# An eight-image convolution and attention kernel on one Trainium2 core: the next image's normalisation moved to GpSimd, and parts of the attention put in another order

## What is computed

```python
x = x + L0(gn(x));  x = x + L1(gn(x))
# L0: N = 2 bottlenecks, C = 256, 4 heads of 64, 1024 positions
t = cbs(x, cv1_w, cv1_bn, 0)                    # 1x1, batch norm, silu
ys = [t[:, :C], t[:, C:]]
for i in range(N):
    yi = ys[-1]
    z = cbs(yi, m_cv1_w[i], m_cv1_bn[i], 1)     # 3x3
    # attention: logits = q.(k + r) / 8, softmax over 1024 keys, times v
    z = bot_attention(z, m_qkv_w[i], m_rw[i], m_rh[i])
    z = silu(bn_eval(conv2d(z, m_cv2_w[i], 0), m_cv2_bn[i]))
    ys.append(yi + z)
return cbs(concatenate(ys, axis=1), cv2_w, cv2_bn, 0)
```

## Time and profile before

| | |
|---|---|
| median of 3 runs | 3366.75 us (3364.51 to 3368.51) |
| the profiled execution, its own time | 3367.39 us |
| its span | 3365.7 us, 1.7 us less than its time |
| mean granted TensorE clock | 0.981 of full speed |
| image 2 begins and ends | 983.65 to 1380.17 us of the span |

### The profile page before, as it was taken

The page is one execution under the profiler, slowest core; times in us unless marked ns, Lnnn a source line. Parts: engine busy times, 40 slices in busy tenths (PEclk is TensorE's granted clock), DMA queues, the critical chain, the costliest instruction groups (busy, mean ns, idle before and its releaser), DMA issues.

```text
span 3365.7 us, 61219 instructions
## 1 busy us (share of the span) xinstructions
PE 3077.0 (91%) x27308; PEld 1574.1 (47%) x27308; DVE 1934.3 (57%) x2575; ACT 1616.3 (48%) x1870; POOL 873.6 (26%) x664
## 2 busy tenths in 40 slices
PE   3779989999999989999999899999899999998997
PEld 3534444454544545444444445445454454445453
DVE  5537565474755656465654757546564657537474
ACT  1315475172733646255651738326462456517382
POOL 1114141041411322132411414113231324014041
PEclk8889999999999999999999999999999999999998
DMA  4200000200011000100001000110001000000001
GB/s 143 73 26 29 1 29 26 78 2 29 11 49 46 2 29 20 57 29 1 30 26 66 14 29 8 38 60 2 29 20 57 29 1 30 26 29 27 1 8 44
DMA packets 35896, 105.61 MB, mean 31 GB/s; under 512 B 12976, under 2 KB 15024, under 8 KB 32944
## 3 DMA queue, kind: packets, MB, share of 16 engines
q1 hardware_dynamic: 35632, 101.69, 8.5%
HBM read 80.18 MB, written 21.50 MB: 30 GB/s over the span
## 4 chain that ended last, share of the span: by engine, by line
PE 70%; DVE 11%; ACT 7%; issue 7%; POOL 4%; DMA 1%; SPq 0%; POOLq 0%; DVEq 0%
PE ps_u L676 42%; PE ps_u L835 12%; DVE row_max L1192 4%; PE ps_o L857 3%; PE ps_o L858 3%; ACT wide L981 3%; PE ps_o L859 3%; PE ps_u L809 3%; ACT ps_u L981 2%; DVE probs L1202 1%; POOL wide L1300 1%; PE ps_u L695 1%; POOL y_pad L1300 1%; ACT probs L985 1%; DVE qk L1181 1%
## 5 line engine op out<-in xcount | busy, mean ns | idle before, releaser
L676 PE MATMUL ps_u<-y_pad,w_c 128*128 128x512 f16 x3456 | 789.5, 386 | 0.0
L1192 DVE TENSOR_REDUCE row_max<-ps_u 128x2 f32<-128x1024 f32 x512 | 619.8, 1221 | 219.6 <-PE ps_u L809 219.3
L1320 POOL TENSOR_TENSOR probs<-wide,probs 128x1024 f16<-128x1024 f32 x224 | 477.2, 2130 | 501.7 <-ACT probs L985 492.4
L676 PEld LDWEIGHTS ps_u<-y_pad,w_c 128*128 128x128 f16 x3456 | 331.3, 98 | 425.2 <-issue 24.2
L1002 DVE SCALAR_TENSOR_TENSOR wide<-wide 128x512 f32<-128x512 f32 x256 | 175.5, 688 | 608.9 <-ACT wide L903 606.7
L835 PE MATMUL ps_u<-qk 64*128 64x512 f16 x3072 | 425.2, 383 | 73.3 <-DVE probs L1202 24.9
L902 ACT ACTIVATE wide<-ps_u,par_m_t 128x512 f32<-128x512 f32 x128 | 99.3, 775 | 758.2 <-PE ps_u L676 758.2
L857 PEld LDWEIGHTS ps_o<-v_ext,probs 128*128 128x128 f16 x4096 | 375.7, 96 | 143.5 <-issue 129.0
L857 PE MATMUL ps_o<-v_ext,probs 128*128 128x65 f16 x4096 | 431.2, 193 | 0.0
L858 PE MATMUL ps_o<-v_ext,probs 128*128 128x64 f16 x4096 | 429.0, 195 | 0.0
L859 PE MATMUL ps_o<-v_ext,probs 128*128 128x65 f16 x4096 | 426.5, 191 | 0.0
(11 more groups left out here) (180 smaller groups left out, 3788.9 us busy)
## 6 DMA issues: line engine op xcount, KB each, us to landing
w_c<-w_c_dram SPq DMA_DIRECT2D x15, 2304.0 KB, 8.9
xn<-in_x_dram SPq DMA_DIRECT2D x32, 512.0 KB, 5.9
o_nat<-in_x_dram SPq DMA_DIRECT2D x64, 256.0 KB, 2.6
out_dram<-qk SPq DMA_DIRECT2D x32, 512.0 KB, 2.7
w_c_dram<-w_c SPq DMA_DIRECT2D x2, 2304.0 KB, 8.0
qk<-in_L_conv_m_cv_w_dram SPq DMA_DIRECT2D x2, 1152.0 KB, 6.9
probs<-in_L_conv_m_cv_w_dram SPq DMA_DIRECT2D x2, 1152.0 KB, 11.1
probs<-in_L_conv_cv_w_dram SPq DMA_DIRECT2D x2, 1024.0 KB, 11.8
```

Source lines behind the costliest of these rows:

```text
L676: ins = e.matmul(o, lhsT, rhs, start=start and k == 0, stop=stop and k == len(pairs) - 1)
L1192: e.reduce_max(row_max[:, g % 2, :, it, half], ps_u[:, use.slot:use.slot + 2, :], axis=AX.X).then_inc(*dve_max.up(i, b, g, half, it))
L1320: e.tensor_tensor(p_part(s, 1), wide[:, w.slot, :], p_part(s, 0), ALU.subtract).then_inc(*pool_lo.up("p", i, b, s))
```

## The change

Four edits, all but the first in the list:
- **norm on GpSimd.** For the images 1 to 7, ScalarE and VectorE skip `norm`; GpSimd follows its scaling (now L1307) by a cast hi (L1311) and a subtraction lo (L1313), each behind a wait for the one before. The `wide` buffer is freed by GpSimd.
- **NORM_PARTS.** In b=0, `gn_mean` moves from behind tile (0,1) to behind tile (1,0), and `gn_var` from behind (1,1) to behind (0,1). In b=1, norms 0 and 1 stand behind (0,0), norm 2 behind (1,0), norm 3 behind (0,1); before, 0 behind (0,0), 1 behind (1,0), 2 and 3 behind (0,1).
- **Projections and first steps.** v 3 and its maxima come ahead of q (0,1); q (1,1) moves from ahead of the steps to behind the logits of step 1; one maximum moves from step 1 to ahead of step 0.
- **Steps 22 and 23** keep the rotation: 22 subtracts on GpSimd, 23 casts and subtracts there.

```diff
@@ norm_ahead
-                plan("norm", i + 1, 0, t, wide_ring.take(("dve_lo", ("norm", i + 1, 0, t))))
+                plan("norm", i + 1, 0, t, wide_ring.take(("pool_lo", ("norm", i + 1, 0, t))))
...
-        NORM_PARTS = {(0, 0, 0): 1, (0, 0, 1): 0, (0, 1, 0): 1, (0, 1, 1): 1, (1, 0, 0): 1, (1, 0, 1): 1, (1, 1, 0): 2, (1, 1, 1): 0}
+        NORM_PARTS = {(0, 0, 0): 1, (0, 0, 1): 1, (0, 1, 0): 1, (0, 1, 1): 0, (1, 0, 0): 2, (1, 0, 1): 1, (1, 1, 0): 1, (1, 1, 1): 0}
         HALF_0 = (("q", 1, 0), ("k", 1, 0), ("v", 0), ("v", 1))
-        HALF_1 = ((("k", 0, 1), 0), (("v", 2), 1), (("k", 1, 1), 1), (("q", 0, 1), 2), (("q", 1, 1), 0))
+        HALF_1 = ((("k", 0, 1), 0), (("v", 2), 1), (("k", 1, 1), 2), (("v", 3), 1), (("q", 0, 1), 0))
...
-            return (("scalar", "vector"), ("scalar", "pool"), ("pool", "pool"))[s % 3 if s < LAST_MAX else 0]
+            return (("scalar", "vector"), ("scalar", "pool"), ("pool", "pool"))[s % 3 if s < LAST_MAX + 2 else 0]
...
                 piece(*at)
                 for _ in range(count):
                     next(maxima)
+                if at == ("v", 3):
+                    next(maxima)
+            plan_shift_row(i, b, 0)
             next(maxima)
-            plan_shift_row(i, b, 0)
-            piece("v", 3)
...
-                if s in (1, 3):
+                if s == 3:
                     next(maxima)
...
                 late = None if w else (i, b, s, use)
+                if s == 1:
+                    piece("q", 1, 1)
@@ tensor, "cv1"
-                        once(dve_lo, "norm", i, 0, t)
+                        once(pool_lo if i else dve_lo, "norm", i, 0, t)
@@ scalar and vector, "norm"
+                    if i and slot == 0:
+                        continue
@@ gpsimd, "norm"
+                    if i and slot == 0:
+                        e.wait_ge(*pool_norm.now())
+                        e.tensor_scalar(xn_parts[:, t, 0, :], wide[:, w.slot, :], 1.0, 0.0, ALU.mult, ALU.add).then_inc(*pool_hi.up("norm", i, slot, t))
+                        e.wait_ge(*pool_hi.now())
+                        e.tensor_tensor(xn_parts[:, t, 1, :], wide[:, w.slot, :], xn_parts[:, t, 0, :],
+                                        ALU.subtract).then_inc(*pool_lo.up("norm", i, slot, t))
```

## The result

| | before | after |
|---|---|---|
| median | 3366.75 us, 5 runs (3364.51 to 3369.06) | 3350.74 us, 5 runs (3349.90 to 3353.16) |
| the profiled execution, its own time | 3367.39 us | 3349.90 us |
| its span | 3365.7 us | 3347.9 us |
| mean granted TensorE clock | 0.981 | 0.984 |

The change takes 16 us away: the ratio is 0.9953, with a 95% interval of 0.9938 to 0.9967.

The account below looks back on a forecast made before the run. TensorE, busy 91% of the span, bounds the kernel, so only its idle time and low-clock stretches count. Gains of 33.5, 17 and 4.6 us less a loss of 51 make 4 us: about 3363 us, range 3352 to 3377.

Parts of the forecast that it names:

- the clock term of part 4: First steps, new order: low clock falling in six places again costs about 1.6 us each, 9.6 us of loss.
- part 4: First steps of 16 bottlenecks, new order: 9.1 us of pace and 5.1 of old falls, less 9.6; gain 4.6 us.
- the slower rival: First steps: two idle times bring the low clock in nearly all 16 bottlenecks; 12 us lost in sum, 3379; chance 0.14.
- The second term: b=0, gn_mean moved: 5.1 us wait for statistics plus 2.2 us low clock, 7.3 us in seven images; loss 51 us.
- My faster rival: No clock fall behind b=0's new wait in most images, first steps pay in full: 3344, half 3354; chance 0.3.
- Part 1: b=1, norm on GpSimd: TensorE's waits for q and k (23.6 us) and low clock (9.9) go; gain 33.5 us.
- GpSimd is late for q: b=1: a norm over 5.7 us on GpSimd makes TensorE wait for tile (1,0) again; 3380 us; chance 0.05.
- Part 3: Steps 22 and 23 on GpSimd: logits of step 24 go 1.07 us sooner in 16 places; gain 17 us.
- the new wait doesn't occur: b=0: something else covers the statistics, so TensorE has no new wait; 3312 us; chance 0.03.
- my three signs of being wrong: Statistics wait under 3 us; GpSimd's cast of tile (1,0) over 12 us after first scaling; low clock costing over 3 us.

Follow-up runs that it names:

- e12: e1 with q (0,1) behind the first shift row instead of ahead of it: 3350.09 us.
- e1: The changed kernel with gn_mean and gn_var of b=0 put back to their old places: 3306.33 us.
- e5: The kernel before the change with only gn_mean and gn_var of b=0 moved as in the change: 3413.15 us.

## Why the prediction was wrong

**The step that failed is the clock term of part 4**: "If the clock falls there, in six places again, a stretch of 3.4 us at the low level costs about 1.6 us instead of 0.86", 9.6 us of loss. It falls in no place. I read the low clock of the earlier trace rows as a property of the place, and took it over to the new order with its count of six. It belonged to the idle times of the old order. The largest of them is the 1.38 us ahead of the shift's product, which q (0,1) now covers, and with q (0,1) moved back (e12) the low clock comes in all 16 places; that this wait alone did it is not shown. I even had it in the rows, and worked out only that the idle total shrinks. The gain of the pace is 0.50 us a place and not 0.57, and the six falls of before cost 4.3 us (0.65 to 0.85 each), not the 5.1 that I took from image 2; the part is 10.3 us measured alone, not 4.6. The same error carries the slower rival, which got 0.14: the late q (1,1) with its two idle times, on which it rested, stands in seven kernels, and the clock falls at none of their 112 places.

**The second term is the stall's size.** Place, releaser, count and the fall in all seven images were right. But I took 7.3 us each; an image pays 6.8, since the wait is 4.94 and not 5.1, and the low stretch, the short one each time, costs 1.9 with the slower product and not 2.2. The edit costs 44 to 47 us (e1, e5), not 51. Together the two terms are 10 to 12 us, and forecast and result lie 12 us apart. My faster rival (3344, or 3354 for half of it) had two clauses: that the first steps pay in full, which came true, and that the clock doesn't fall behind the new wait in most images, where it fell in all seven. So its range holds the result with one reason right and one wrong, and that is partly luck.

**Part 1 was right**: 34.2 us (some 5 each way) for 33.5, the 9.9 us of clock behind the wait included, and GpSimd was on time for q with 1.6 us to spare (forecast 1.35). The rival "GpSimd is late for q" falls.

**Part 3 was right**: 15.6 for 17, with three low stretches more in the images of that kernel than in the one before; without them a place gives 1.14 us. In the change itself the logits of step 24 come 1.18 us sooner behind the transposed tile.

**The rival "the new wait doesn't occur" fell**, though its 3312 us are near what e1 shows when the wait is taken out (3306).

So the picture of large effects that nearly cancel stands; the balance was read 12 us too dear, with both errors mostly in the low clock and on the same side. The range went down only to the middle of the faster rival, and the two errors together went just past it. Of my three signs of being wrong none came (the wait is 4.94 us, GpSimd's cast of tile (1,0) ends 10.5 us after the first scaling starts, the low clock costs 1.9 us at a wait): none of them looked for the low clock staying away.

## What to carry to other kernels

A low clock seen at a place need not belong to the place: here, when an edit covered the largest of the idle times that stood there, the low clock went from all 144 places, so an old count must not be carried over to a new order. Before a product that needs another engine's result is moved forward, compare the time at which the result is there with the time at which the product would be reached, for a queue of matmuls behind it pays in full: here one position in a table cost 45 us and hid most of a good change. Of an edit with several parts that cancel, run the parts.

## What the runs showed of the hardware

**VectorE and GpSimd hold each other up.** VectorE in b=1 after, the product of a tile's two passes (both inputs in SBUF):

```profile
1176.26 0.69 DVE L1007 SCALAR_TENSOR_TENSOR wide<-wide 128x512 f32<-128x512 f32 x1 [6.36 <-ACT wide L906]
1177.68 0.69 DVE L1178 TENSOR_TENSOR z<-wide,z 128x512 f16<-128x512 f32 x1 [0.73 <-POOL z L1322]
1180.22 0.80 DVE L1007 SCALAR_TENSOR_TENSOR wide<-wide 128x512 f32<-128x512 f32 x1 [1.85 <-ACT wide L906]
...
1192.12 1.58 DVE L1007 SCALAR_TENSOR_TENSOR wide<-wide 128x512 f32<-128x512 f32 x1 [3.29 <-ACT wide L906]
```

The product takes 0.69 us alone. At 1192.12 it took 1.58: GpSimd's subtraction shown above ran from 1191.03 to 1193.16, and the product ended 0.54 us behind it. At 1180.22 the product was first, and GpSimd's subtraction took 2.44 us instead of 2.13. By the Trainium skill (SBUF — State Buffer, section "Who interferes with whom") such a pair exclude each other and the later is blocked; in the prediction I had found no row of a blocked VectorE, and the case at 1192.12 agrees with that rule. Which of the two is the later can't always be read from the starts: at 1177.68 VectorE's subtraction began 0.05 us behind GpSimd's scaling (1177.63, above) and took its usual 0.69 us, while the scaling took 1.73, against 1.19 at 1183.00 with VectorE idle. Here it cost nothing, since the tile had time.

**The low clock answers to small changes.** The same wait of 4.94 us was followed by 0.82, 0.71 or, with some idle time in it, 0.58 in the next 8 us, depending on kernel and image; and identical idle times at the first steps were followed by a low stretch in image 2 and by none in image 5 of the kernel before.
